# Local attention in a two-layer decoder: who writes the mask band into the score banks

## Chip, core and metric
The kernel runs on one core of a Trainium2 chip. The metric is the device time of one execution in microseconds (us); lower is better. The names of the engines here are those of the profile: PE is TensorE (PEld its weight loads), ACT is ScalarE, DVE is VectorE, POOL is GpSimd, SP is SyncE.

## What is computed
The reference is two decoder layers over 16 sequences of 128 tokens and 256 features: attention, retention and a spline layer, then local attention, cross attention and a mixture of experts. Only the fourth, the local attention with a window of 64, is touched:

```python
qkv = jnp.einsum('bse,fe->bsf', x, w_qkv)             # 16 heads of 16 features
scores = jnp.einsum('bhnid,bhnjd->bhnij', qc, kc) * scale
band = (j >= i) & (j <= i + C)
scores = jnp.where(mask[None, None], scores, jnp.finfo(scores.dtype).min)
probs = jax.nn.softmax(scores, axis=-1)
out = jnp.einsum('bhnij,bhnjd->bhnid', probs, vc)
```

In the kernel a query row sees the keys from 64 rows behind it to itself: `band` is a 128x128 tile that holds 0 there and -1e30 elsewhere. Scores are added onto it.

## The kernel before
`phase_window` works in 32 ticks, `TICKS = 2 * B`. A tick `h` is half of one sequence's 16 heads: 8 score tiles of 128x128, four in each of two PSUM banks (a bank holds 128 partitions x 512 float32). Even ticks use banks `SC[0]` and `SC[1]`, odd ticks `SC[2]` and `SC[3]`. `s` is 0 or 1 for the bank within the tick. Four ticks serve a pair of sequences, and `p = h % 4` says which step of preparing the next pair is taken beside them (transposing x, then projecting q, k and v).

Each engine has a written program of its own, and order is kept by semaphores. In tick `h`, in this order:

- PE: `score(h)`: the band into both banks' share (below), then 12 small matmuls that add q times k on top; `weigh(h-3)`, `transpose_p(h-2, 0)`, the preparation of step `p`, `transpose_p(h-2, 1)`.
- DVE: `invert(h-1, 0)`, `take_PT(h-3, 1)`, `find_max(h)` over both banks, `take_PT(h-2, 0)`, `invert(h-1, 1)`, then what is left of preparation, residual sums and statistics. `finish_part` (three times) is a chain of small operations for the norm.
- ACT: a preparation copy, `exps(h-1, 1)`, in some ticks `round_oT`, `exps(h, 0)`, `lay_band(h-1)`. One `exps` is four exponentials of 128x128, each with a row sum, which shows as an ACTIVATE and an ACTIVATION_READ_ACCUMULATOR.
- POOL: scales the probabilities of both banks by the inverse sums.

The band gets into a bank in two ways. For `s = 0` PE multiplies the identity with `band` (line 1930, bfloat16, 512 columns); for `s = 1` ACT copies `band` into the bank (line 1709) from tick 2 on. ACT may write a bank only when the exponentials have read it, and `score(h)` may start only when `exps_done` and `band_laid` of tick `h-2` are there. ACT's copy for tick `h-1` stands behind `exps(h, 0)`, and `exps(h, 0)` needs `find_max(h)`.

Of the kernel before, what the change touches and what calls it, by code (L numbers as in the profile page):

```python
# [9 lines left out]
ACT = mybir.ActivationFunctionType  # L10
# [13 lines left out]
def wait(eng, sem, value):  # L24

    if isinstance(value, int) and value <= 0:
        return
    eng.wait_ge(sem, value)
# [1078 lines left out]
def flat(ap):  # L1107
    return ap.rearrange("p h n -> p (h n)")
# [420 lines left out]
def phase_window(nc, a, sem, sb_, bank, X, ident, mean, var_eps, rstd, minus_half, stats, ln_tmp, banks, w, kept, ahead_loaded, n_ahead):  # L1529

    local = ExitStack()
    with local:
        def sb(name, shape, dt=F32):
            return sb_(name, shape, dt, local)

        NH, DH = 16, 16
        PAIRS, TICKS = B // 2, 2 * B
# [8 lines left out]
        band = sb("win_band", [128, 4, 128], BF16)  # L1546
        ident_b = sb("win_ident_b", [128, 128], BF16)
# [48 lines left out]
        exps_done = sem("win_exps_done")  # L1596
        band_laid = sem("win_band_laid")
# [14 lines left out]
        PREP, SC, PTB, OT = bank[0:2], bank[2:6], bank[6], bank[7]  # L1612
# [3 lines left out]
        with nc.Block() as block:  # L1616
# [39 lines left out]
            def _(act):  # L1656
# [26 lines left out]
                def take_v(i):  # L1683
                    act.wait_ge(v_projected, i + 1)
                    if i >= PAIRS:
                        nc.scalar.activation(cr_V[:, i - PAIRS].rearrange("p i d -> p (i d)"), PREP[(i + 1) % 2], ACT.Copy).then_inc(V_ready, 1)
                        return
                    wait(act, weighed, 8 * (i - 1))

                    values = PREP[(i + 1) % 2] if i > 0 else OT  # L1690
                    for ql in range(2):
                        src = values.rearrange("p (h l a d) -> p h l a d", l=2, a=2, d=DH)[:, :, ql]
                        dst = V[:, i % 2].rearrange("p b (h l a) d -> p (b h) l a d", l=2, a=2)[:, :, ql, :, DH * ql:DH * ql + DH]
                        ins = nc.scalar.activation(dst, src, ACT.Copy)
                    ins.then_inc(V_ready, 1)

                def exps(h, s):
                    act.wait_ge(max_found, h + 1)
                    wait(act, p_transposed, 2 * (h - 2) + s + 1)
                    for i in range(4):  # L1700
                        at = 4 * s + i
                        ins = nc.scalar.activation(P[:, h % 2, s, i, :], SC[2 * (h % 2) + s][:, i * 128:(i + 1) * 128], ACT.Exp,  # L1702
                                                   bias=neg_max[:, h % 2, at:at + 1], accum_out=exp_sum[:, h % 2, at:at + 1])
                    ins.then_inc(exps_done, 1)


                def lay_band(h):
                    act.wait_ge(exps_done, 2 * h + 2)
                    nc.scalar.activation(SC[2 * (h % 2) + 1].rearrange("p (h n) -> p h n", n=128), band[:], ACT.Copy).then_inc(band_laid, 1)

                def round_oT(i):
                    act.wait_ge(weighed, 8 * i + 8)
                    wait(act, out_projected, i)
                    nc.scalar.activation(oT_hi[:].rearrange("p c b n -> p b c n"), OT.rearrange("p (b c n) -> p b c n", b=2, c=2), ACT.Copy).then_inc(oT_hi_ready, 1)
# [11 lines left out]
                for h in range(TICKS + 5):  # L1726
                    m, p = h // 4, h % 4
                    if p == 0 and 0 < m < PAIRS + CROSS:
                        take_v(m)
                    if p > 0 and m + 1 < PAIRS + CROSS and h != 1:  # L1730
                        (round_xT, round_q, round_k)[p - 1](m + 1)
                    if 0 <= h - 1 < TICKS:
                        exps(h - 1, 1)
                    if p == 2 and m >= 1:
                        round_oT(m - 1)
                    if h < TICKS:
                        exps(h, 0)
                    if 0 <= h - 1 < TICKS - 2:
                        lay_band(h - 1)

            @block.vector
            def _(dve):
# [119 lines left out]
            def _(pe):  # L1862
# [62 lines left out]
                def score(h):  # L1925
                    i, j, hf = h // 4, h // 2 % 2, h % 2
                    wait(pe, exps_done, 2 * (h - 1))

                    for s in range(2 if h < 2 else 1):
                        nc.tensor.matmul(SC[2 * (h % 2) + s], ident_b[:], flat(band[:]), start=True, stop=True)  # L1930
                    wait(pe, band_laid, h - 1)
                    if h % 4 == 0:
                        pe.wait_ge(q_lo_ready, i + 1)
                        pe.wait_ge(k_lo_ready, 2 * i + 2)
                    for k in range(KD):
                        for lhs, rhs in ((q_hi, k_lo), (q_lo, k_hi), (q_hi, k_hi)):
                            for s in range(2):
                                rows = slice(32 * (2 * hf + s), 32 * (2 * hf + s) + 32)
                                ins = nc.tensor.matmul(SC[2 * (h % 2) + s][:, k * 256:(k + 1) * 256], lhs[rows, i % 2, k, j, :],
                                                       rhs[rows, i % 2, k, j].rearrange("p a n -> p (a n)"), start=False, stop=True, skip_group_check=True)  # L1940
                    ins.then_inc(scored, 1)
# [33 lines left out]
                for h in range(TICKS + 5):  # L1975
                    m, p = h // 4, h % 4

                    if h < TICKS:
                        score(h)
                    if 0 <= h - 3 < TICKS:  # L1980
                        weigh(h - 3, 0)
                        weigh(h - 3, 1)
                    if 0 <= h - 2 < TICKS:
                        transpose_p(h - 2, 0)
                    if p == 0 and 0 <= m - 2 < PAIRS:
                        project_out(m - 2)
                    if m + 1 < PAIRS + CROSS:
                        (transpose_x, project_q, project_k, project_v)[p](m + 1)
                    if 0 <= h - 2 < TICKS:
                        transpose_p(h - 2, 1)  # L1990
# [906 lines left out]
```

## Time and profile before

| what | value |
|---|---|
| median of 3 runs | 1028.16 us (1028.05 to 1029.35) |
| span of the profiled execution, first to last instruction | 1025.7 us |
| PE busy over the span | 973.5 us, 95% |
| ACT busy over the span | 744.1 us, 73% |
| DVE busy over the span | 753.1 us, 73% |
| the ticks that lay bands, first exponential to behind the last copy | 665.87 to 804.80 us of the span |

The profiled execution's own time is its span; what lies around the span in a timed run is known only from the difference of the two, 1028.16 - 1025.7 = 2.5 us. Starts and durations of ACT and DVE are observed. Ends of PE rows are modelled, so that overlapping matmuls make PE look busier than its array is. Busy times are unions: two overlapping instructions count once.

### The profile page before, as it was taken

Reading aid. Unit: us, or ns where it says so; the run is one execution under the profiler, and the core shown is the slowest. Engines: PE = TensorE matmul, PEld = TensorE weight load, DVE = VectorE, ACT = ScalarE, POOL = GpSimd, SP = SyncE. Lnnn points to the kernel's source line nnn. Section 1 sums busy time; section 2 is a strip of 40 time slices with the busy share of each in tenths; the row PEclk is TensorE's granted clock in tenths of the full one; section 3 lists DMA queues with packets and bytes.
Section 4 is the critical chain, followed back from the end, with each engine's and each line's share of the span. In section 5 each row is a group of like instructions: output and inputs, shape, how many; then the busy total and the mean of one; then the engine's idle time right before and its main releaser. Section 6 shows DMA issues by size and latency. Waiting matters only on the chain. (4 is left out here: it accounts for less than half of the span.)

```text
span 1025.7 us, 19312 instructions
## 1 busy us (share of the span) xinstructions
PE 973.5 (95%) x6855; PEld 806.4 (79%) x6855; DVE 753.1 (73%) x1495; ACT 744.1 (73%) x2052; POOL 351.9 (34%) x306
## 2 busy tenths in 40 slices
PE   8899999999999999999998987889999999899997
PEld 4788888998899989988987876767778789774444
DVE  5888867667677676666757889879998644567774
ACT  5889877878778887777763348698999645558882
POOL 2242333333333333332320120266655310107672
PEclk9999999999999999999999998999999999999999
DMA  6321000000000001000205000000000000028652
GB/s 206 104 62 62 1 2 1 1 2 1 1 2 1 1 1 37 1 1 1 83 4 147 1 1 1 1 2 2 2 3 2 2 1 1 8 73 264 219 183 83
DMA packets 31840, 40.21 MB, mean 39 GB/s; under 512 B 8192, under 2 KB 23296, under 8 KB 31744
## 3 DMA queue, kind: packets, MB, share of 16 engines
q1 hardware_dynamic: 31744, 38.98, 12.2%
q8 instruction: 55, 0.90, 0.4%
q14 instruction: 41, 0.34, 0.1%
HBM read 36.74 MB, written 2.23 MB: 38 GB/s over the span
## 5 line engine op out<-in xcount | busy, mean ns | idle before, releaser
L354 POOL TENSOR_TENSOR roped_q<-roped_q,sin_q 128x512 f32<-128x512 f32 x64 | 81.8, 1279 | 270.6 <-DVE sin_q L518 270.6
L354 POOL TENSOR_TENSOR roped_k<-roped_k,sin_k 128x512 f32<-128x512 f32 x64 | 82.4, 1287 | 65.2 <-DVE sin_k L518 65.2
L1702 ACT ACTIVATE win_P<-banks,win_neg_max 128x128 f32<-128x128 f32 x256 | 91.3, 389 | 13.2 <-DVE win_neg_max L1789 13.0
L421 ACT ACTIVATE P<-banks,neg_max 128x128 f32<-128x128 f32 x256 | 90.1, 370 | 9.1 <-DVE neg_max L536 9.1
L464 ACT ACTIVATE oT_hi<-banks,bv_col 128x512 fp32r<-128x512 f32 x64 | 44.1, 689 | 58.0 <-PE banks L684 58.0
L1635 POOL TENSOR_TENSOR win_P<-win_P,win_inv 128x512 f32<-128x512 f32 x64 | 66.5, 1040 | 56.9 <-DVE win_inv L1794 56.8
L517 DVE SCALAR_TENSOR_TENSOR roped_k<-banks,qk_bias,cos 128x512 f32<-128x512 f32 x64 | 48.0, 750 | 51.3 <-ACT sin_k L430 51.0
L539 DVE SCALAR_TENSOR_TENSOR oT_lo<-banks,bv_col,oT_hi 128x512 fp32r<-128x512 f32 x64 | 47.9, 749 | 47.5 <-ACT oT_hi L464 47.5
L430 ACT ACTIVATE sin_q<-banks 64x512 f32<-64x512 f32 x128 | 75.9, 593 | 3.7 <-PE banks L37 1.4
L430 ACT ACTIVATE sin_k<-banks 64x512 f32<-64x512 f32 x128 | 75.8, 592 | 3.1 <-PE banks L37 0.8
L684 PE MATMUL banks<-PT,V 128*128 128x128 f32 x512 | 72.0, 284 | 5.6 <-ACT PT L448 5.5
L644 PE MATMUL banks<-WO_lo,oT_hi 128*128 128x256 f32 x256 | 72.9, 285 | 0.0
L644 PE MATMUL banks<-WO_hi,oT_lo 128*128 128x256 f32 x256 | 71.5, 279 | 0.0
L644 PE MATMUL banks<-WO_hi,oT_hi 128*128 128x256 f32 x256 | 71.5, 279 | 0.0
L684 PEld LDWEIGHTS banks<-PT,V 128*128 128x128 f32 x512 | 62.0, 191 | 7.7 <-ACT PT L448 7.5
L659 PE MATMUL banks<-roped_k,roped_q 128*128 128x128 f32 x512 | 67.7, 275 | 0.0
L659 PEld LDWEIGHTS banks<-roped_k,roped_q 128*128 128x128 f32 x512 | 62.3, 192 | 0.3 <-issue 0.2
L2576 DVE TENSOR_TENSOR moe_hidden<-banks,moe_squared 128x512 f32<-128x512 f32 x64 | 44.1, 689 | 24.4 <-POOL moe_squared L2457 21.8
L517 DVE SCALAR_TENSOR_TENSOR roped_q<-banks,qk_bias,cos 128x512 f32<-128x512 f32 x64 | 48.0, 750 | 16.5 <-ACT sin_q L430 16.1
L1702 ACT ACTIVATION_READ_ACCUMULATOR win_P<-banks,win_neg_max 128x1 f32 x256 | 58.4, 228 | 0.0
L448 ACT ACTIVATE PT<-banks 128x512 f32<-128x512 f32 x64 | 38.2, 598 | 22.5 <-PE banks L634 22.0
L421 ACT ACTIVATION_READ_ACCUMULATOR P<-banks,neg_max 128x1 f32 x256 | 53.9, 210 | 0.0
(436 smaller groups left out, 3168.3 us busy)
## 6 DMA issues: line engine op xcount, KB each, us to landing
ret_V<-moe_gate_rows SPq DMA_DIRECT2D x16, 512.0 KB, 4.9
ctx<-moe_gate_rows SPq DMA_DIRECT2D x16, 512.0 KB, 5.1
X<-in_x SPq DMA_DIRECT2D x4, 512.0 KB, 6.4
stage<-in_wqT SPq DMA_DIRECT2D x4, 512.0 KB, 4.2
stage<-in_wvT SPq DMA_DIRECT2D x4, 512.0 KB, 6.2
stage<-in_woT SPq DMA_DIRECT2D x4, 512.0 KB, 4.3
ctx<-in_ctxT SPq DMA_DIRECT2D x4, 512.0 KB, 6.1
out<-X SPq DMA_DIRECT2D x8, 256.0 KB, 2.4
```

What stands on the lines that cost most here:

```text
L354: nc.gpsimd.tensor_tensor(roped[w][:, p, :], roped[w][:, p, :], sin_part[w][:], ALU.add).then_inc(roped_sum[w], 1)
L421: ins = nc.scalar.activation(P[:, i, :], SC[:, i * 128:(i + 1) * 128], ACT.Exp, bias=neg_max[:, r % 2, i:i + 1], accum_out=exp_sum[:, r % ...
L430: ins = nc.scalar.activation(sin_part[w][64 * half:64 * half + 64, :], QK[w][64 * (1 - half):64 * (2 - half), :], ACT.Copy)
L464: nc.scalar.activation(flat(oT_hi[:]), PO[:], ACT.Identity, bias=bv_col[:, (r - 2) % HEADS0:(r - 2) % HEADS0 + 1]).then_inc(oT_hi_ready, 1)
L517: nc.vector.scalar_tensor_tensor(per_batch(roped[w][:, p, :]), per_batch(QK[w][:]), qk_bias[:, w, r:r + 1], table(cos), ALU.add, ALU.mult) ...
L539: nc.vector.scalar_tensor_tensor(flat(oT_lo[:]), PO[:], bv_col[:, (r - 3) % HEADS0:(r - 3) % HEADS0 + 1], flat(oT_hi[:]).bitcast(F32), ALU ...
L644: ins = nc.tensor.matmul(OUT[i // 2][:, i % 2 * D:(i % 2 + 1) * D], lhs[:, i, :], rhs[:, ur, :], start=ur == 0 and i % 2 == 0 and lhs is o ...
L659: ins = nc.tensor.matmul(SC[:, i * 128:(i + 1) * 128], roped[0][:, p, toks], roped[1][:, p, toks], start=False, stop=True, skip_group_chec ...
L684: ins = nc.tensor.matmul(PO[:, i * 128:(i + 1) * 128], V[:, ur // 4 % 2, i, h * 128:(h + 1) * 128], PT[:, i, :], start=True, stop=True)
L1635: nc.gpsimd.tensor_tensor(some, some, inv[:, h % 2, 4 * s:4 * s + 4].rearrange("p (h n) -> p h n", n=1).broadcast_to([128, 4, 128]), ALU.m ...
L1702: ins = nc.scalar.activation(P[:, h % 2, s, i, :], SC[2 * (h % 2) + s][:, i * 128:(i + 1) * 128], ACT.Exp, bias=neg_max[:, h % 2, at:at + ...
L2576: TT(dst, up_bank(s), squared[:, s % 4, :], ALU.mult).then_inc(hidden_done, 1)
```

## The change
ACT copies the band into both banks of every tick from 2 on, each copy directly behind the exponentials that read the bank. PE lays the band for ticks 0 and 1 alone, where it did for all 32 ticks in bank `s = 0`.

```diff
-                def lay_band(h):
-                    act.wait_ge(exps_done, 2 * h + 2)
-                    nc.scalar.activation(SC[2 * (h % 2) + 1].rearrange("p (h n) -> p h n", n=128), band[:], ACT.Copy).then_inc(band_laid, 1)
+                def lay_band(h, s):
+                    act.wait_ge(exps_done, 2 * h + s + 1)
+                    nc.scalar.activation(SC[2 * (h % 2) + s].rearrange("p (h n) -> p h n", n=128), band[:], ACT.Copy).then_inc(band_laid, 1)
...
                     if 0 <= h - 1 < TICKS:
                         exps(h - 1, 1)
+                    if 0 <= h - 1 < TICKS - 2:
+                        lay_band(h - 1, 1)
                     if p == 2 and m >= 1:
                         round_oT(m - 1)
                     if h < TICKS:
                         exps(h, 0)
-                    if 0 <= h - 1 < TICKS - 2:
-                        lay_band(h - 1)
+                    if h < TICKS - 2:
+                        lay_band(h, 0)
...
-                    for s in range(2 if h < 2 else 1):
-                        nc.tensor.matmul(SC[2 * (h % 2) + s], ident_b[:], flat(band[:]), start=True, stop=True)
-                    wait(pe, band_laid, h - 1)
+                    if h < 2:
+                        for s in range(2):
+                            nc.tensor.matmul(SC[2 * (h % 2) + s], ident_b[:], flat(band[:]), start=True, stop=True)
+                    else:
+                        pe.wait_ge(band_laid, 2 * h - 2)
```

ACT's program over the end of one tick with `p = 3` and the start of the next, before (L1702 an exponential, L1709 a copy of the band, L1679 and L1694 preparation copies of k and v; a wait stands with the instruction that holds it):

```order
L1679 ACTIVATE win_k_hi<-banks,win_parity 128x4x128
L1702 ACTIVATE win_P,win_exp_sum<-banks,win_neg_max 128x128 [waits win_p_transposed,win_max_found]
L1702 ACTIVATE win_P,win_exp_sum<-banks,win_neg_max 128x128 x3
L1702 ACTIVATE win_P,win_exp_sum<-banks,win_neg_max 128x128 [waits win_p_transposed,win_max_found]
L1702 ACTIVATE win_P,win_exp_sum<-banks,win_neg_max 128x128 x3
L1709 ACTIVATE banks<-win_band 128x512 [waits win_exps_done]
L1694 ACTIVATE win_V<-banks 128x8x2x16 [waits win_weighed,win_v_projected]
```

The same place in the changed kernel:

```order
L1679 ACTIVATE win_k_hi<-banks,win_parity 128x4x128
L1702 ACTIVATE win_P,win_exp_sum<-banks,win_neg_max 128x128 [waits win_p_transposed,win_max_found]
L1702 ACTIVATE win_P,win_exp_sum<-banks,win_neg_max 128x128 x3
L1709 ACTIVATE banks<-win_band 128x512 [waits win_exps_done]
L1702 ACTIVATE win_P,win_exp_sum<-banks,win_neg_max 128x128 [waits win_p_transposed,win_max_found]
L1702 ACTIVATE win_P,win_exp_sum<-banks,win_neg_max 128x128 x3
L1709 ACTIVATE banks<-win_band 128x512 [waits win_exps_done]
L1694 ACTIVATE win_V<-banks 128x8x2x16 [waits win_weighed,win_v_projected]
```

There is a second copy in the tick, and each copy's wait is now for the exponentials in the row above it; before, it was for the group of four ahead of that one.

PE's program at the start of a tick, before (L1947 the last transposes of the tick ahead, L1930 the band, L1939 the scores):

```order
L1947 MATMUL banks<-ident,win_P 128x128 x3
L1930 MATMUL banks<-win_band,win_ident_b 128x512 [waits win_exps_done]
L1939 MATMUL banks<-win_k_lo,win_q_hi 128x256 [waits win_band_laid]
L1939 MATMUL banks<-win_k_lo,win_q_hi 128x256
L1939 MATMUL banks<-win_k_hi,win_q_lo 128x256 x2
```

And in the changed kernel, where four lines more stand ahead of each number:

```order
L1951 MATMUL banks<-ident,win_P 128x128 x3
L1943 MATMUL banks<-win_k_lo,win_q_hi 128x256 [waits win_band_laid,win_exps_done]
L1943 MATMUL banks<-win_k_lo,win_q_hi 128x256
L1943 MATMUL banks<-win_k_hi,win_q_lo 128x256 x2
```

The band's matmul is gone, and both waits stand with the first score matmul.

## Rows read from the trace of the kernel before

**Rows 1.** The page: its first line, and PE in part 1
```profile
span 1025.7 us, 19312 instructions
...
PE 973.5 (95%) x6855; PEld 806.4 (79%) x6855; DVE 753.1 (73%) x1495; ACT 744.1 (73%) x2052; POOL 351.9 (34%) x306
```

**Rows 2.** Busy time in two stretches: all band-laying ticks, and four late ticks
```profile
core 0: us, PE busy (x) PEld busy (x) DVE busy (x) ACT busy (x) POOL busy (x), PEclk, DMA share, GB/s
665.87:804.80 138.93, 128.96 (x1444) 105.54 (x1440) 122.25 (x256) 126.01 (x569) 81.78 (x89) 0.99 0.01 2
751.28:769.17 17.89, 17.38 (x201) 14.29 (x200) 16.48 (x38) 16.77 (x76) 8.32 (x8) 1.00 0.01 3
```

**Rows 3.** Who waited for whom, 655 to 820 us
```profile
engine line waited for: us in total, times, longest us
...
PEld banks L1939 <- ACT banks L1709: 16.5, 29, 1.9
ACT win_P L1702 <- DVE win_neg_max L1789: 13.0, 20, 1.4
...
DVE win_neg_max L1789 <- PE banks L1939: 8.1, 14, 1.4
```

**Rows 4.** ACT in order of time, 761 to 770 us
```profile
761.56 0.41 ACT L1702 ACTIVATE win_P<-banks,win_neg_max 128x128 f32<-128x128 f32 x1
...
762.81 0.37 ACT L1702 ACTIVATE win_P<-banks,win_neg_max 128x128 f32<-128x128 f32 x1 [0.74 <-DVE win_neg_max L1789]
...
767.27 0.37 ACT L1702 ACTIVATE win_P<-banks,win_neg_max 128x128 f32<-128x128 f32 x1
...
768.31 0.37 ACT L1702 ACTIVATE win_P<-banks,win_neg_max 128x128 f32<-128x128 f32 x1
768.56 0.21 ACT L1702 ACTIVATION_READ_ACCUMULATOR win_P<-banks,win_neg_max 128x1 f32 x1
768.65 0.61 ACT L1709 ACTIVATE banks<-win_band 128x512 f32<-128x512 bf16 x1
769.17 0.70 ACT L1679 ACTIVATE win_k_hi<-banks,win_parity 128x512 fp32r<-128x512 f32 x1
```

**Rows 5.** PE, then DVE, then PE in order of time, 764 to 770 us
```profile
764.86 0.38 PE L1939 MATMUL banks<-win_k_lo,win_q_hi 32*128 32x256 f32 x2 [0.18 <-ACT banks L1709]
...
765.36 0.17 DVE L1794 RECIPROCAL win_inv<-win_exp_sum 128x4 f32<-128x4 f32 x1
765.45 0.66 DVE L1799 COPY win_PT<-banks 128x512 f32<-128x512 f32 x1
766.02 1.21 DVE L1789 TENSOR_REDUCE win_neg_max<-banks 128x8 f32<-128x1024 f32 x1
...
768.88 0.38 PE L1930 MATMUL banks<-win_band,win_ident_b 128*128 128x512 bf16 x1
769.32 0.38 PE L1939 MATMUL banks<-win_k_lo,win_q_hi 32*128 32x256 f32 x2
```

**Rows 6.** Groups by line in the stage, 655 to 820 us
```profile
L1709 ACT ACTIVATE banks<-win_band 128x512 f32<-128x512 bf16 x30 | 18.5, 618 | 0.0
...
L1930 PE MATMUL banks<-win_band,win_ident_b 128*128 128x512 bf16 x34 | 12.6, 380 | 0.6 <-ACT win_P L1702 0.6
```

**Rows 7.** ACT and DVE at 667 us; ACT in the last phase
```profile
666.91 0.37 ACT L1702 ACTIVATE win_P<-banks,win_neg_max 128x128 f32<-128x128 f32 x1
667.16 0.21 ACT L1702 ACTIVATION_READ_ACCUMULATOR win_P<-banks,win_neg_max 128x1 f32 x1
667.25 0.38 ACT L1702 ACTIVATE win_P<-banks,win_neg_max 128x128 f32<-128x128 f32 x1
...
667.40 0.18 DVE L1794 RECIPROCAL win_inv<-win_exp_sum 128x4 f32<-128x4 f32 x1 [0.63 <-ACT win_P L1702]
...
909.23 0.60 ACT L2481 ACTIVATE moe_relu<-banks 128x512 f32<-128x512 f32 x1 [0.36 <-PE banks L37]
909.86 0.63 ACT L2486 ACTIVATE moe_squared<-moe_relu 128x512 f32<-128x512 f32 x1
...
933.59 1.09 ACT L2481 ACTIVATE moe_relu<-banks 128x512 f32<-128x512 f32 x2 [0.48 <-PE banks L2687]
```

## The prediction, made before the changed kernel ran
> **What bounds the kernel now.** I began with the page. PE is busy 95% of the span of 1025.7 us [rows 1], which invites the reading that TensorE is the bound everywhere. But only the local attention is touched, so I took the busy times of its ticks alone, then who waits for whom there, then single rows in order of time. In the 138.93 us in which bands are laid, PE is busy 128.96, ACT 126.01, DVE 122.25 [rows 2]: no engine is clearly alone. The waits tell more. PE's weight loads for the scores sit 16.5 us, in 29 of 30 ticks, until ACT's copy of the band has ended. ACT sits 13.0 us, 20 times, until the maxima are there. DVE sits 8.1 us until the scores are there [rows 3]. Three engines wait for each other in a ring, and that ring is what sets a tick.
>
> Its length can be read off one turn. The scores start at 764.86; find_max starts at 766.02, 1.16 later, and the exponentials that it frees start at 767.27, 1.25 after that [rows 4, 5]. Four exponentials take until the copy of the band starts at 768.65, 1.38 later. The next scores start at 769.32, 0.67 behind the copy's start. The sum is 1.16 + 1.25 + 1.38 + 0.67 = 4.46 us; four ticks take 17.89 us [rows 2], which is 4.47 each. So one turn of the ring is one tick. What makes the ring so short-linked is ACT's order: the copy for tick h-1 stands behind the exponentials of tick h.
>
> ACT is close behind as a bound of its own. In those four ticks it is busy 16.77 of 17.89 us [rows 2].
>
> **What the change does, part by part.**
>
> *The ring opens.* The copy for tick h-1 no longer stands behind exps(h, 0). The scores of tick h+1 then need only exps(h-1, 1) and its copy, which ACT does ahead of exps(h, 0). PE can do them while ACT is still busy with a whole group of exponentials, and the maxima can be there early. DVE's part between the end of one exps(h-1, 0) and the next maxima is 0.09 for the inverse, 0.57 for the copy of PT and 1.25 for the maxima [rows 5], 1.9 us, or 2.5 with one more 128x512 operation such as that copy. ACT has in that time two copies of the band and a group of exponentials, at least 0.52 + 1.38 + 0.52 = 2.4 us, and a preparation copy on top, about 3 us or more. So ACT should almost never wait for maxima, and 13 us of waiting can go.
>
> *What ACT idles now, in starts.* Idle between rows understates what can be filled, since instructions without a wait overlap. The last exponential before a wait starts at 761.56. Exponentials follow each other in 0.34 us (666.91 to 667.25 in [rows 7]), so ACT could have gone on at 761.90; it did at 762.81, 0.91 later, where the row says 0.74 idle [rows 4]. Each wait hides 0.17 more. Idle in the band-laying ticks is 138.93 - 126.01 = 12.9 us [rows 2]; with about 20 waits at 0.17 it is 12.9 + 3.4 = 16.3 us. This is all that the opened ring can give.
>
> *What ACT gets.* 30 more copies of 128x512. One lasts 0.618 us on average [rows 6], but the next instruction starts 0.52 behind it (768.65 to 769.17) [rows 4]. 30 x 0.52 = 15.6 us.
>
> *The wait for its own exponentials.* Each of the 60 copies now waits for the instruction directly ahead of it on the same engine. Before, the copy started at 768.65, while the last read of the accumulator ran from 768.56 to 768.77 [rows 4]: it did not wait for that one. Now it must. No such copy is in the trace, so I bound the price by the nearest rows. DVE, which waits for exactly this signal, starts at 667.40, where ACT itself went on at 667.25: 0.15 [rows 7]. In the last phase ACT squares what it has just rectified, with a wait for itself: rectify at 909.23, square at 909.86, 0.63 apart, where two rectifications without a wait are 1.09 - 0.60 = 0.49 apart: 0.14 [rows 7]. The end of the accumulator read, 768.77, with the 0.03 that 909.86 lies behind the end of the row ahead of it (909.83), gives 0.15 over the start seen. The lower bound is nothing, if the wait were hidden in the queue; the upper is about 0.2, where a group's reads end later because exponentials ran without a pause. I take 0.15: 60 x 0.15 = 9.0 us. The first 30 copies pay it too, though they were there before.
>
> What a page says of this stands apart. The Trainium skill, ScalarE: Activation LUTs, section "What ACT_TABLE_LOAD costs", says that back-to-back ACTIVATEs overlap by about 93 ns. If a self-wait lost only that overlap, the price by the page would be 60 x 0.093 = 5.6 us and the change 3.4 us cheaper than by the rows. The rows of this trace show 0.60 - 0.49 = 0.11 of overlap and 0.03 more behind a wait, so I stay with them.
>
> *What PE loses.* 30 matmuls of at most 0.38 us [rows 6], 11.4 us at the very most, and the waits. PE is not what ACT waits for once the ring is open; with ACT full, this saving is cover and worth nothing. PE's clock is granted in full in the four late ticks at 17.38 busy of 17.89 (1.00) and at 0.99 over all [rows 2]; it gets a little less work per us, and I take no loss for it.
>
> *What remains of the waits.* Some of ACT's waits come from DVE being long busy (the longest is 1.4 us [rows 3], at the chains of statistics). I leave 1 us in all for those.
>
> *The sum.* 15.6 + 9.0 + 1.0 - 16.3 = +9.3 us. Checked on four late ticks: idle there is 1.12 + 2 x 0.17 = 1.5, work 16.4, added 4 x 0.52 + 8 x 0.15 = 3.3, so 19.7 us in place of 17.89, 0.45 a tick; early ticks wait more now and lose less. ACT's last tick is followed by the same tail, so the stage's loss is the kernel's. Against the profiled execution it is 1025.7 + 9.3 = 1035.0 us of span, and 2.5 us lie around it: 1037.5 us, against the median of 1028.16.
>
> **Rivals.**
>
> *The self-wait costs nothing.* Then the sum is 15.6 + 1.0 - 16.3 = +0.3 us: 1028.5, no change. For it speaks that the copies waited before without any visible idle time (0.0 in [rows 6]), against it that this wait was for a group 1.38 us older, and that both nearest pairs of rows show 0.14 to 0.15. It decides below (2.06 - 0.3) / 60 = 0.03 us a copy. This is the case that ends on the other side, not slower.
>
> *TensorE was the bound after all.* Then 30 band matmuls fall off the path at 0.38 or less and the waits for the copies with them; at 0.3 each it is -9 us: 1019 us. For it speaks PE's 17.38 of 17.89 us; against it that its loads sit idle 16.5 us for the copies and are busy only 14.29 [rows 2, 3]. The Trainium skill, Trainium Kernel Development and Optimization, section "Best Practices", says that matmul busy time does not judge the distance to the roof and the share of weight loads does; the trace agrees, 80% against 97% in the same stretch. And ACT, given 24.6 us of new starts, has 16.3 free.
>
> *The waits for maxima stay.* If DVE, which has its own 16.48 of 17.89 us, keeps the maxima as late relative to ACT as now, nothing is filled and the cost is 15.6 + 9.0 = +24.6: 1052.8. Half filled, it is 1045. For it speaks DVE's busy share and that invert(h-1, 0) stands ahead of find_max(h) in its program, so that the maxima can't run further ahead than one group; against it the slack worked out above. A drop of PE's granted clock would come out here too.
>
> **How the numbers follow.** What a measurement of this kernel can tell from no change is about 0.2%, 2.06 us. The forecast, ACT full with self-waits of 0.09 to 0.2 us, spans 60 x 0.09 = 5.4 to 12 us for them, and 0 to 3 us of waits left: +4.7 to +14.3, 1033 to 1042.5. I give it 0.72. Self-wait free or nearly so: 0.12. TensorE the bound: 0.04. Waits stay to half or more: 0.12. The range of 1031 to 1043.5 leaves out the last, the free wait and the rare one, in part, about 2 in 10. Faster: 0.05. Within 0.2%: 0.11. Slower: 0.84.
>
> **What would show it.** The stage's ticks grow from 4.47 to about 4.9 us late, and ACT is busy nearly all of them. ACT's wait for the maxima falls from 13.0 to 1 or 2 us. PE's wait for the copies stays in the rows but no longer matters, or moves to another name, and DVE's idle time grows. Copies start 0.49 us behind the start of the last exponential, not 0.34. The forecast is wrong if the copies start at 0.34, or if ACT still waits 10 us for maxima.

## The result, and the profile after

The changed kernel takes 1038.75 us (median of 4 runs, 1037.99 to 1039.99) beside 1028.76 us for the kernel before on the same chip: ratio 1.0095, 95% interval 1.0082 to 1.0109, 10.0 us slower. 1037.5 was forecast, with 1031 to 1043.5 as the range.

Who waited for whom in the stage, 655 to 835 us, of the changed kernel (columns as in [rows 3]):

```profile
engine line waited for: us in total, times, longest us
...
PEld banks L1963 <- DVE win_PT L1801: 16.5, 22, 1.8
DVE win_inv L1796 <- ACT win_P L1702: 13.5, 24, 1.6
...
PEld banks L1943 <- issue: 10.8, 27, 1.4
...
PEld banks L1943 <- ACT win_P L1702: 3.5, 4, 2.2
...
PE banks L1943 <- ACT banks L1709: 2.7, 2, 2.0
...
ACT win_P L1702 <- DVE win_neg_max L1791: 0.3, 1, 0.3
DVE win_neg_max L1791 <- PE banks L1943: 0.2, 1, 0.2
```

ACT's wait for the maxima has gone from 13.0 us in 20 turns [rows 3] to 0.3 in one. The weight loads of the scores no longer wait for a copy, where they waited 16.5 us [rows 3]. They still idle 10.8 us for nothing that the profile shows, and 3.5 for exponentials; PE's own wait for the copies is 2.7 us, and was 4.7:

```profile
PE banks L1939 <- ACT banks L1709: 4.7, 13, 1.6
```

DVE now waits 13.5 us for ACT's exponentials, which was 4.3 before, and PE's loads wait 16.5 us for DVE's copies of PT, which was 6.8. The ring is open; PE waits for DVE, DVE for ACT, and ACT for almost nothing.

Busy time of the changed kernel, in the stretch from its first exponential to behind the exponentials of tick 30, the place in the program where [rows 2] ends, and in four late ticks:

```profile
core 0: us, PE busy (x) PEld busy (x) DVE busy (x) ACT busy (x) POOL busy (x), PEclk, DMA share, GB/s
667.56:816.20 148.64, 129.87 (x1434) 106.52 (x1430) 123.84 (x258) 146.39 (x599) 82.67 (x90) 0.97 0.01 2
777.25:796.90 19.65, 17.51 (x204) 13.96 (x196) 16.29 (x31) 19.40 (x81) 10.17 (x10) 1.00 0.01 2
```

ACT is busy 19.40 of 19.65 us; four late ticks take 19.65 where 19.7 was forecast and 17.89 was the time before [rows 2]. DVE, busy 16.29 us, and PE, busy 17.51, do in 19.65 us about what they did in 17.89.

ACT of the changed kernel in order of time, over one copy behind exponentials:

```profile
779.26 0.22 ACT L1702 ACTIVATION_READ_ACCUMULATOR win_P<-banks,win_neg_max 128x1 f32 x1
779.35 0.39 ACT L1702 ACTIVATE win_P<-banks,win_neg_max 128x128 f32<-128x128 f32 x1
779.60 0.23 ACT L1702 ACTIVATION_READ_ACCUMULATOR win_P<-banks,win_neg_max 128x1 f32 x1
779.86 0.60 ACT L1709 ACTIVATE banks<-win_band 128x512 f32<-128x512 bf16 x1
780.40 0.35 ACT L1702 ACTIVATE win_P<-banks,win_neg_max 128x128 f32<-128x128 f32 x1
...
781.43 0.37 ACT L1702 ACTIVATE win_P<-banks,win_neg_max 128x128 f32<-128x128 f32 x1
781.68 0.21 ACT L1702 ACTIVATION_READ_ACCUMULATOR win_P<-banks,win_neg_max 128x1 f32 x1
781.92 0.60 ACT L1709 ACTIVATE banks<-win_band 128x512 f32<-128x512 bf16 x1
```

The reader is to see where the accumulator's last read ends, 779.83 and 781.89, and that the copy starts 0.03 behind it. From the last exponential to the copy it is 0.51 and 0.49 us; without the wait it was 0.34 [rows 4]. So the wait costs 0.15 to 0.17.

The span grew by 10.8 us. Between the first and the last exponential of the stage it is 144.15 us before (665.87 to 810.02) and 153.23 after (667.56 to 820.79), +9.1. The other 1.7 lie ahead of the stage, in instructions that the change doesn't touch, and they go with PE's granted clock. It is at the lower of its two levels, half speed, for 17.1 us ahead of the stage in this execution and 10.2 in the one before, in stretches of 3.4 us or twice that. The added one nearest to the stage, before and then after:

```profile
609.50:612.90 3.40, 2.80 (x32) 2.36 (x31) 3.30 (x20) 1.94 (x3) 0.66 (x1) 1.00 0.00 0
...
609.50:612.90 3.40, 3.40 (x18) 3.40 (x18) 3.33 (x18) 0.32 (x3) 0.00 (x0) 0.50 0.00 0
```

PE is busy in all 3.40 us of it; at half speed that leaves 1.7 us of work over. I compare stages below by the time from first to last exponential, which leaves this out. It does not leave out such stretches within the stage: their total there is 3.4 us before, 10.2 in the changed kernel, 0 in e1, e5, e6, e8 and e10, 3.4 in e2, e4 and e7, 6.8 in e3, 10.2 in e11, and 19 in e9a and e9b.

### The profile page after: what moved, and what is told of

Read it like the earlier page. It is cut to its first block and busy times, and to the rows that moved or that the text cites. A ratio compares the mean times of both kernels' runs of the same rounds, so it can differ in the third digit from the quotient of the medians.

```text
span 1036.5 us, 19312 instructions
## 1 busy us (share of the span) xinstructions
PE 976.1 (94%) x6825; PEld 809.1 (78%) x6825; DVE 753.8 (73%) x1495; ACT 765.2 (74%) x2082; POOL 352.7 (34%) x306
## 5 line engine op out<-in xcount | busy, mean ns | idle before, releaser
L1702 ACT ACTIVATE win_P<-banks,win_neg_max 128x128 f32<-128x128 f32 x256 | 90.2, 370 | 0.6 <-DVE win_neg_max L1791 0.3
L1702 ACT ACTIVATION_READ_ACCUMULATOR win_P<-banks,win_neg_max 128x1 f32 x256 | 53.7, 210 | 0.0
```

## Experiments

The column "stage" gives that time from the first to the last exponential, read from each profile. The kernel before ran beside each group of kernels, with medians of 1028.3 to 1029.0 us, and the ratios are taken to those runs.

| kernel | bands laid in ticks from 2 on | us | ratio to before, 95% | stage us |
|---|---|---|---|---|
| before | PE one, ACT one, late | 1028.76 | | 144.15 |
| changed | ACT two, directly behind | 1038.75 | 1.0082 to 1.0109 | 153.23 |
| e1_early_copy | PE one, ACT one, directly behind | 1024.86 | 0.9951 to 0.9976 | 140.04 |
| e2_late_copies | ACT two, each a group later | 1033.30 | 1.0031 to 1.0061 | 148.72 |
| e3_no_self_wait | ACT two, behind the next exponential | 1032.70 | 1.0023 to 1.0053 | 148.51 |
| e4_band_twice | changed, PE's matmul put back | 1037.41 | 1.0070 to 1.0100 | 152.59 |
| e5_one_copy_no_self_wait | PE one, ACT one behind the next exponential | 1025.68 | 0.9960 to 0.9980 | 141.06 |
| e6_pe_both | PE two | 1025.12 | 0.9954 to 0.9978 | 141.78 |
| e7_half_band | ACT one as e1, none for `s = 0` (half of the scores stay without a band) | 1021.67 | 0.9923 to 0.9950 | 138.86 |
| e8_add_later | e1, `add_out` a tick later | 1026.71 | 0.9972 to 0.9990 | 141.48 |
| e9a_more_dve_early | e1, more work on DVE | 1037.23 | 1.0070 to 1.0101 | 151.78 |
| e9b_more_dve_after | changed, more work on DVE | 1039.92 | 1.0095 to 1.0122 | 153.57 |
| e10_add_later_no_self_wait | e5, `add_out` a tick later | 1028.22 | 0.9993 to 1.0010 | 143.24 |
| e11_wait_for_copy | changed, a wait behind each copy | 1043.89 | 1.0140 to 1.0168 | 159.51 |

**Was TensorE the bound?** e4 puts the band's matmul back into the changed kernel.

```diff
                         pe.wait_ge(band_laid, 2 * h - 2)
+                        nc.tensor.matmul(SC[2 * (h % 2)], ident_b[:], flat(band[:]), start=True, stop=True)
```

> The changed kernel with TensorE's 30 band matmuls put back: TensorE lays the band in bank s = 0 once more behind ScalarE's copy, ahead of the scores, which changes no value. My account: TensorE has slack, so no change against the changed kernel, 1038.8 within 1 us. Rival, TensorE's matmul work is on the path and the change saved it: 30 x 0.21 to 0.31 = 6 to 9 us slower, 1045 to 1048.

1037.41 us, 1.3 less than the changed kernel, a little outside the 1 us that I allowed, and its stage is 0.6 us shorter: 30 matmuls cost nothing there. Saving them gained nothing either, and the rival falls. Most of the 0.6 is one period of four ticks (from the maxima of tick 20 to those of tick 24), which took 20.09 us in the changed kernel and 19.65 in e4. The changed kernel's clock is at half speed there for 3.4 us, from 763.1, and e4's isn't.

**What does a self-wait cost?** e11 adds one behind every copy, and changes neither work nor order.

```diff
                     nc.scalar.activation(SC[2 * (h % 2) + s].rearrange("p (h n) -> p h n", n=128), band[:], ACT.Copy).then_inc(band_laid, 1)
+                    act.wait_ge(band_laid, 2 * h + s + 1)
```

> The changed kernel with one wait more behind each of the 60 copies: ScalarE's next instruction waits until the copy is complete. Order and work are as in the changed kernel. If a self-wait costs what lies between the overlapped start and the end of the row ahead plus 0.03 us: a copy lasts 0.60, the next row now starts 0.54 behind its start, so 0.63 - 0.54 = 0.09 us each, 60 x 0.09 = 5.4 us: about 1044. If self-waits are free in a queue that is always full: 1038.8.

1043.89 us, 5.1 more than the changed kernel, so 5.1 / 60 = 0.086 us a wait; by the stage it is 159.51 - 153.23 = 6.3, or 0.10 each. ACT of this kernel in order of time:

```profile
779.77 0.60 ACT L1709 ACTIVATE banks<-win_band 128x512 f32<-128x512 bf16 x1
780.40 1.27 ACT L1679 ACTIVATE win_k_hi<-banks,win_parity 128x512 fp32r<-128x512 f32 x2
...
783.10 0.60 ACT L1709 ACTIVATE banks<-win_band 128x512 f32<-128x512 bf16 x1
783.73 0.37 ACT L1702 ACTIVATE win_P<-banks,win_neg_max 128x128 f32<-128x128 f32 x1
```

What follows the copy starts 0.63 behind the copy's start, the 0.60 of the copy and 0.03; in the changed kernel it was 0.54 (779.86 to 780.40). The wait is paid in full where ACT is the bound. The Trainium skill, ScalarE: Activation LUTs, section "What ACT_TABLE_LOAD costs", gives about 93 ns for the overlap of two ACTIVATEs. The copies of the kernel before overlap by that (0.618 less 0.52); those of the changed kernel by 0.06 (0.60 less 0.54), and the price of a wait behind them is this overlap and the 0.03 that the next instruction starts behind their end, 0.09 together. Behind exponentials with an accumulator the wait costs 0.16, since the accumulator's read ends later than the exponential's own successor could start.

**The same copies without the wait.** e2 puts each copy a group later, e3 behind the first exponential of the next group (`copy` names the tick and bank).

```diff
# e2
-                        lay_band(h - 1, 1)
+                        lay_band(h - 1, 0)
...
-                    if h < TICKS - 2:
-                        lay_band(h, 0)
+                    if 0 <= h - 1 < TICKS - 2:
+                        lay_band(h - 1, 1)
# e3
                         ins = nc.scalar.activation(P[:, h % 2, s, i, :], SC[2 * (h % 2) + s][:, i * 128:(i + 1) * 128], ACT.Exp,
                                                    bias=neg_max[:, h % 2, at:at + 1], accum_out=exp_sum[:, h % 2, at:at + 1])
+                        if i == 0 and copy is not None and 0 <= copy[0] < TICKS - 2:
+                            lay_band(*copy)
```

> The changed kernel with each of ScalarE's copies one group of exponentials later, so that none waits for the row ahead of it; the last copy stands behind exps(h, 0), as before the change. My account: no self-waits, so 9.7 us cheaper than the changed kernel at best, but the ring of before is closed again and leaves some idle: 1029 to 1035, with some waits for the maxima back. Rival, self-waits are free and only the copies' 0.52 us count: not faster than the changed kernel, 1038.8 or more.

> The changed kernel with each copy moved behind the first exponential of the next group: same 60 copies, no wait for the row directly ahead, and the ring still open but for one exponential. My account: 60 x 0.16 = 9.7 us off the changed kernel, so about 1029, and copies followed and preceded at 0.34 and 0.52 us. Rival, self-waits are free: 1038.8 as the changed kernel.

e2 came inside its range, 1033.30. e3 missed: 1032.70, 6.1 us less than the changed kernel where 9.7 were expected. The self-waits are gone (copies start 0.34 behind the exponential, and what follows a copy 0.52 behind it), but ACT waits for the maxima again, in e3:

```profile
ACT win_P L1702 <- DVE win_neg_max L1789: 2.7, 8, 0.9
```

Counted in starts (what lies over 0.34 us from one exponential to the next), the pauses are 5.8 us in e3 and 0.4 in the changed kernel, where what lies over 0.54 between a copy and the exponential behind it adds 0.5. The stage's account closes: 9.4 for the self-waits and 1.0 for the shorter distance behind copies are gone, some 5.6 of pauses are new (0.7 of them ahead of preparation copies), and the stage is 4.7 us shorter. My reading is that what the self-waits took, they also gave: time for DVE to be ready. No run separates this from the later place of the copies.

**The ring alone.** e1 is the kernel before with its one copy ahead of `exps(h, 0)`.

```diff
                         exps(h - 1, 1)
+                    if 0 <= h - 1 < TICKS - 2:
+                        lay_band(h - 1)
                     if p == 2 and m >= 1:
                         round_oT(m - 1)
                     if h < TICKS:
                         exps(h, 0)
-                    if 0 <= h - 1 < TICKS - 2:
-                        lay_band(h - 1)
```

> The kernel before, with one thing changed: ScalarE's copy (bank s = 1 only) stands directly behind the exponentials that read the bank, ahead of exps(h, 0). TensorE still lays the other bank. My account (the ring opens, ScalarE's own work is the bound, a copy that waits for the row ahead costs 0.16 us): 30 x 0.16 = 4.8 us added, up to 16.3 us of idle filled, about 1 us of it left: -10.5 us against before, about 1018; ScalarE's wait for the maxima near 1 us. Rival, VectorE keeps the maxima late: no change, 1028.8, wait for the maxima still about 13 us. Rival, TensorE's work is the bound: no change either, with its loads busy throughout.

1024.86 us: 3.7 less than before, not 10.5. It beats both kernels, but the expected size was far off. Its self-waits cost 5.6 us over 30 copies, where 4.8 were expected, and ACT's wait for the maxima is still 4.2 us in 10 turns. The stage is 4.1 us shorter. By periods from the maxima of one tick to those of the fourth behind it, 1.3 of this lie in ticks 0 to 4, 2.2 in ticks 4 to 20 and 0.3 in ticks 20 to 28. Late ticks hardly changed: from tick 21 to 25 it is 17.90 us in both kernels, from 25 to 29 17.77 before and 17.47 in e1. A part of the 3.7 goes with the clock: the kernel before has 3.4 us at half speed in ticks 0 to 4 of its profiled execution and e1 none, and where executions had the same mean granted clock, 0.992, the kernel before took 1027.3 to 1028.0 and one of e1 1025.1.

Something else gives the late ticks their length, and two theories were put up: A, ScalarE's own program, and B, TensorE's.

e5 frees ACT of its self-waits, e6 of all copies, e7 frees PE of its band.

```diff
# e5: lay_band(h - 1) behind the first exponential of exps(h, 0)
-                        exps(h, 0)
-                    if 0 <= h - 1 < TICKS - 2:
-                        lay_band(h - 1)
+                        exps(h, 0, h - 1)
# e6
-                    if 0 <= h - 1 < TICKS - 2:
-                        lay_band(h - 1)
...
-                    for s in range(2 if h < 2 else 1):
+                    for s in range(2):
...
-                    wait(pe, band_laid, h - 1)
# e7, on e1; in each half of bank s = 0 the first of the three products overwrites what is there
-                    for s in range(2 if h < 2 else 1):
+                    for s in range(2 if h < 2 else 0):
...
-                                                       rhs[rows, i % 2, k, j].rearrange("p a n -> p (a n)"), start=False, stop=True, skip_group_check=True)
+                                                       rhs[rows, i % 2, k, j].rearrange("p a n -> p (a n)"), start=(h >= 2 and s == 0 and lhs is q_hi and rhs is k_lo), stop=True, skip_group_check=True)
```

> The kernel of the early-copy run, with ScalarE's one copy a tick moved behind the first exponential of exps(h, 0), so that it waits for no row directly ahead. Theory A, the early-copy run is held by ScalarE's own work: 30 x 0.19 = 5.6 us faster than it, about 1019. Theory B, with the ring open TensorE's own work (band matmul and its full program, about 17.9 us for four late ticks) is the next bound there: within 2 us of the early-copy run, about 1024, and late ticks still 17.9 us for four.

> The kernel before without any copy of ScalarE's: TensorE lays the band in both banks of every tick. Nothing waits for a copy, and ScalarE is freed of 15.6 us. Theory B (TensorE next in line): four late ticks take about 17.9 + 4 x 0.21 to 0.31 = 18.8 to 19.1 us, so 30 x 0.25 = 7 us over the early-copy run, about 1031. Theory A (ScalarE next in line): faster than the early-copy run, 1015 or less.

> The early-copy run's kernel with TensorE's 30 band matmuls left out and nothing in their place: from tick 2 on, bank s = 0 gets no band, so the output differs. ScalarE's program is as in the early-copy run. Theory B: TensorE's late ticks get 4 x 0.21 to 0.31 us shorter, down to ScalarE's own 17.2 for four: 3 to 6 us faster than the early-copy run, about 1020. Theory A: no change, 1024.9.

e5 at 1025.68 and e6 at 1025.12 refute A: ACT got 5.6 and 15.6 us less to do than in e1, and nothing came of it. They do not leave all of B either. e6 has 30 matmuls of PE more than e1, and its stage is 1.7 us longer where B asked for 7; e7 has 30 fewer, and its stage is 1.2 us shorter. The medians say the same where the mean granted clock is the same, 0.995: 1021.5 to 1021.7 for e7, 1022.9 for e1, 1025.0 and 1025.2 for e6. (e7's 3.2 us between medians is within the 3 to 6 that B expected, but it holds executions of different clocks.) So a band matmul of PE costs 0.04 to 0.06 us of the stage here, not the 0.21 to 0.31 that B put on it. Busy times of e7, e1 and e6, with no, one and two band matmuls a tick, from the maxima of tick 21 to those of tick 25 and on to those of tick 29:

```profile
759.14:777.03 17.89, 16.64 (x207) 14.06 (x196) 16.52 (x38) 17.28 (x78) 9.88 (x9) 1.00 0.01 2
777.03:794.22 17.19, 16.55 (x208) 14.05 (x196) 15.62 (x32) 16.80 (x77) 8.32 (x8) 1.00 0.01 1
...
760.16:778.06 17.90, 17.20 (x206) 14.31 (x204) 16.52 (x38) 17.32 (x78) 9.89 (x9) 1.00 0.01 2
778.06:795.53 17.47, 16.99 (x206) 14.37 (x204) 15.65 (x32) 17.08 (x77) 8.33 (x8) 1.00 0.01 1
...
759.43:777.50 18.07, 17.86 (x204) 14.71 (x211) 16.64 (x38) 15.00 (x72) 9.89 (x9) 1.00 0.01 2
777.50:795.40 17.90, 17.69 (x204) 14.77 (x210) 15.70 (x31) 14.99 (x72) 8.32 (x8) 1.00 0.01 2
```

The first period is 17.9 to 18.1 us with ACT at 15.00 to 17.32 and PE at 16.64 to 17.86. What is common to them is DVE, busy 16.5 to 16.6. In the second period DVE is busy 15.6 to 15.7 in all three, and the length follows PE's matmuls, 0.3 to 0.4 us for four of them. Waits of DVE in e1, then e6, then e7:

```profile
782.13 1.23 DVE L1789 TENSOR_REDUCE win_neg_max<-banks 128x8 f32<-128x1024 f32 x1 [0.44 <-PE banks L1939]
...
781.85 1.22 DVE L1787 TENSOR_REDUCE win_neg_max<-banks 128x8 f32<-128x1024 f32 x1 [0.64 <-PE banks L1936]
...
790.61 1.23 DVE L1787 TENSOR_REDUCE win_neg_max<-banks 128x8 f32<-128x1024 f32 x1 [0.50 <-PE banks L1936]
...
793.18 0.69 DVE L1807 TENSOR_TENSOR X<-banks,X 128x512 f32<-128x512 f32 x1 [0.64 <-PE banks L37]
...
772.38 1.23 DVE L1789 TENSOR_REDUCE win_neg_max<-banks 128x8 f32<-128x1024 f32 x1 [0.50 <-PE banks L1939]
...
774.95 0.69 DVE L1809 TENSOR_TENSOR X<-banks,X 128x512 f32<-128x512 f32 x1 [0.64 <-PE banks L37]
```

The 0.50 for scores that PE can start only behind DVE's own split of k, and the 0.64 for `project_out`, stand in e6 and in e7. The wait for the scores of tick 26 is 0.64 with two band matmuls, 0.44 with one and under 0.1 with none. Theory C: DVE's program, with its waits through PE, sets the late ticks, some 17.9 us for four, and PE's matmuls count only as far as they lengthen such a wait.

**Is it DVE?** e9a and e9b give DVE two more operations a pair of sequences, in e1 and in the changed kernel.

```diff
+                    wait(dve, q_lo_ready, i)
+                    for spare_at in range(2):
+                        nc.vector.scalar_tensor_tensor(spare[:, spare_at], PREP[(i + 1) % 2], scale, wide(q_hi[:, i % 2]).bitcast(F32),
+                                                       ALU.mult, ALU.subtract)
```

> The early-copy kernel with VectorE doing its q split three times, twice into a spare tile that nothing reads: 2 more operations of about 0.57 us for each pair, 16 in all. Theory C: VectorE's program is the bound, so 14 to 16 x 0.57 = 8 to 9 us slower than the early-copy run, about 1033. Rival, VectorE has slack there: 1025.

> The changed kernel with the same 16 operations more on VectorE. If ScalarE alone sets its 19.65 us for four late ticks, VectorE's 17.9 has 1.75 us of slack for the 1.15 us put in, and the time stays near 1038.8, within 2 us. If VectorE counts there too, 8 to 9 us slower, 1047.

In e1 it costs 12.4 us, in the changed kernel 1.2. But the 12.4, where 8 to 9 were expected, are not DVE's work alone. Two of e9a's periods of four ticks, from maxima to maxima:

```profile
763.17:783.57 20.40, 19.06 (x204) 15.75 (x206) 17.81 (x39) 17.48 (x77) 9.88 (x9) 0.92 0.01 1
783.57:802.25 18.68, 17.37 (x204) 14.42 (x207) 16.74 (x33) 17.35 (x77) 8.28 (x8) 1.00 0.01 2
```

In e1 they take 17.92 and 17.47 us. In the second, at full clock, the 1.25 us of new work cost 1.21, as C says. The first costs 2.5, and in it PE's clock is at half speed for 3.4 us. DVE and then PE in e9a, and the same product of PE in e1:

```profile
774.17 1.25 DVE L1778 SCALAR_TENSOR_TENSOR win_spare<-banks,win_q_hi 128x512 bf16<-128x512 f32 x2
...
782.42 0.69 DVE L1804 COPY win_PT<-banks 128x512 f32<-128x512 f32 x1 [1.24 <-PE banks L1952]
...
779.20 0.41 PE L37 MATMUL banks<-win_w_hi,win_xT_hi 128*128 128x256 f32 x1
779.41 0.41 PE L35 MATMUL banks<-win_w_lo,win_xT_hi 128*128 128x256 f32 x1
...
770.21 0.28 PE L37 MATMUL banks<-win_w_hi,win_xT_hi 128*128 128x256 f32 x1
770.33 0.29 PE L35 MATMUL banks<-win_w_lo,win_xT_hi 128*128 128x256 f32 x1
```

PE's matmuls for v start 0.21 apart in place of 0.12, the transposes behind them are late, and DVE waits 1.24 us for those. Just ahead of that PE is busy 2.87 of 4.00 us (774 to 778) and waits for DVE. Whether DVE's added work brings the lower clock isn't shown, but it is there in all of e9a: all four executions have a mean granted clock of 0.982 to 0.984, those of e1 0.991 to 0.995. The four periods of e9a that hold such a stretch are 2.1 to 2.8 us longer than e1's, the three that hold none 0.35, 0.43 and 1.21. So late ticks have no slack on DVE, early ones have some, and by an estimate from these periods (9.8 us longer in the four, less 0.35 to 1.25 for the work in each) some 5 to 8 of the 12.4 us go with the clock. In the changed kernel as much time at half speed (e9b, 19 us) and the same added work cost 1.2 us together: there DVE and PE both have slack.

**Can its wait be taken away?** e8 moves `add_out`, with its 0.64, one tick on; e10 does the same in e5.

```diff
-                    if p == 0 and 0 <= m - 2 < PAIRS:
-                        add_out(m - 2)
...
+                    if p == 1 and 0 <= m - 2 < PAIRS:
+                        add_out(m - 2)
                     if p == 1 and 0 < m < PAIRS + CROSS - 1:
                         split_xT(m + 1)
```

> The early-copy kernel with one residual addition a pair of sequences, add_out, moved on VectorE from the end of a tick with p = 0, where it waits 0.64 us for project_out, to the next tick, ahead of split_xT. Theory C: with the ring open, the next bound is VectorE's own program with its waits through TensorE, 17.9 us for four late ticks in every kernel so far but those that ScalarE holds; the wait of 0.64 us goes and four late ticks take about 17.3: 7 x 0.64 = 4.5 us faster than the early-copy run, about 1020.5. Rival, something else sets 17.9, or the addition, now ahead of find_max, costs what it saved: no change or slower, 1025 or more.

> The kernel with one copy a tick behind the first exponential of the next group, and add_out moved as in the run with the later addition. ScalarE's own program is then 16.4 us for four late ticks instead of 17.2. Theory C: like the run with the later addition, about 1020 to 1021, since ScalarE is not the bound in either; if ScalarE's self-waits begin to count at 17.3, up to 3 us faster than it.

e8 is 1.9 us slower than e1, e10 2.5 slower than e5. The wait did not go; DVE of e8 in the tick where `add_out` had been:

```profile
775.43 0.18 DVE L1794 RECIPROCAL win_inv<-win_exp_sum 128x4 f32<-128x4 f32 x1 [0.87 <-ACT win_P L1702]
776.08 0.69 DVE L1799 COPY win_PT<-banks 128x512 f32<-128x512 f32 x1 [0.47 <-PE banks L1947]
```

In place of 0.64 for the projection it waits 0.87 for the exponentials and 0.47 for the transposes, and the addition still has to be done, now ahead of the maxima. So the gain that I expected fell, and the rival that I had named, no change or slower, came in both: the 0.64 was cover for other work that is not ready sooner. How much of the loss is that and how much the addition's new place, no run tells.

## Why the prediction was right

**The ring opens.** Right in the changed kernel, where ACT's wait for the maxima is 0.3 us and not 13.0. Not right as a statement on what bounded the kernel before. That one turn is 4.46 us beside 4.47 proves nothing: its four distances run from one tick's scores to the next tick's, and so add up to a tick whatever holds it. One link of that turn wasn't tight. The maxima at 766.02 carry no wait for the scores; they stand 0.57 behind DVE's copy at 765.45 [rows 5], and DVE comes to that from its statistics without a pause:

```profile
763.37 0.72 DVE L1814 BATCH_NORM_STATS2 stats<-X 128x6 f32<-128x256 f32 x2
764.13 0.47 DVE L51 TENSOR_TENSOR ln_tmp<-stats 128x8 f32<-128x8 f32 x1
...
765.28 0.17 DVE L61 TENSOR_SCALAR var_eps<-ln_tmp 128x8 f32<-128x8 f32 x1
```

From 760.35 to 770.38 no row of DVE carries a wait, so in these ticks DVE's own program was the bound. The ring can have been the bound only in others, where DVE waited for the scores, 14 of them [rows 3]. e1, with the ring open and nothing else changed, keeps 17.90 us from tick 21 to 25. I named one loop where DVE's own program lay on top of it.

**What ACT idles, 16.3 us, all to be filled.** Right for this change, since ACT got more than the others needed. The size held too: in starts, what lies over 0.34 us from one exponential to the next adds up to 16.9 us before and 0.4 after. As a gain by itself it would have been wrong by most of it: e1 brought 3.7, e6, with ACT freed of all copies, 3.8.

**30 copies at 0.52.** Held: the stage's own sum is 15.6 + 60 x 0.16 - 16.3 = 8.9 us, and 9.1 were measured between first and last exponential. That it came so close is in part luck. Behind a copy that has waited, the next instruction starts 0.54 later and not 0.52, 1.0 us over 60 copies that the prediction doesn't have; of the 1 us that it left for remaining waits, 0.3 came; and some 0.4 us is the one period with a stretch at half clock.

**60 self-waits at 0.15.** The term that decided the sign. It was 0.16 on average (the 60 distances between last exponential and copy add up to 9.4 us over 0.344 each). e11 shows that such waits are paid in full here, and e2 and e3 that without them the copies cost 4 to 5 us over the kernel before, still slower. So the rival "the self-wait costs nothing", with 1028.5, had a second error in it: where the self-waits were taken out, part of ACT's waits for the maxima came back.

**PE's saving is worth nothing.** Shown by e4 for the changed kernel. Rivals "TensorE was the bound" and "the waits stay" both fell, the second by the first waits table above.

**The clock.** In the four late ticks of the busy times it is 1.00 before and after. Over the stage it is 0.99 before and 0.97 after, 10.2 us at half speed in place of 3.4. I took no loss for it. ACT hid most of it, and 0.4 us shows, in the one period of 20.09 us. Ahead of the stage it made the 1.7 us by which the span grew beyond 9.1.

**Around the span.** 2.5 us was too much. The profiled execution of the changed kernel took 1038.32 us with a span of 1036.5, so 1.8 lie around it. The 2.5 set a median beside the span of one execution; where an execution of the kernel before had the same span, 1025.7, in a later run, it took 1027.46. The forecast span, 1035.0, was 1.5 us short, and the time 1.25. Whether the 0.9 us between the stage's 9.1 and the medians' 10.0 are the stage or the clock ahead of it, no run tells.

**Left open.** Which waits through PE lengthen DVE's 15.6 to 16.6 us of work to 17.2 to 18.1 in four late ticks was read from rows, and the two attempts to remove one (e8 and e10) moved it. What sets the early ticks of e1, where DVE has slack, was not tried. Nor was it tried what brings PE's clock down.

## What to carry to other kernels

An instruction that waits for the one directly ahead on its own engine gives up their overlap, 0.09 to 0.16 us here; count it at each place, and see whether something independent can stand between. Idle time of an engine is what new work may fill, not what a shorter loop gives back: before a gain is promised, find the next loop of nearly the same length, and note that the same idle shows up under another name when it is removed. The distances around a loop add up to its period whether it is the bound or not; what tells is a wait at every link. A saving on an engine that waits already was worth nothing in the changed kernel, and a fifth of what B put on it in e1, though PE had looked 97% busy. And before a cost is put down to added work, compare the granted clock of the two executions.

## What the runs showed of the hardware that was not expected

Exponentials that run without a pause grow longer in the profile: 0.370 us on average in the changed kernel, where each group is followed by a self-wait, 0.389 before, 0.424 in e2 and 0.457 in e3, though they start at the same 0.34 us distance. Within e3 they last 0.36 right behind a pause and up to 0.61 after forty or more instructions without one. The rows of the lines for e3 and after:

```profile
L1702 ACT ACTIVATE win_P<-banks,win_neg_max 128x128 f32<-128x128 f32 x256 | 100.2, 457 | 3.1 <-DVE win_neg_max L1789 2.7
...
L1702 ACT ACTIVATE win_P<-banks,win_neg_max 128x128 f32<-128x128 f32 x256 | 90.2, 370 | 0.6 <-DVE win_neg_max L1791 0.3
```

Busy time of ACT is therefore no measure of what it has to do: 100.2 us and 90.2 us for the same 256 exponentials. Distances between starts are.
